# Graph attention on one core: the last chunk of 32 slots is prepared behind all adds of the chunk in front of it

## What is computed

```python
def _gat(x, src, dst, W, a_src, a_dst, b):
    n = x.shape[0]
    xw = (x @ W).reshape(n, H, FH)
    al_s = jnp.einsum('nhf,hf->nh', xw, a_src)
    al_d = jnp.einsum('nhf,hf->nh', xw, a_dst)
    e = jax.nn.leaky_relu(al_s[src] + al_d[dst], NEG_SLOPE)
    m = jax.ops.segment_max(e, dst, num_segments=n)
    ee = jnp.exp(e - m[dst])
    den = jax.ops.segment_sum(ee, dst, num_segments=n)
    alpha = ee / den[dst]
    out = jax.ops.segment_sum(alpha[:, :, None] * xw[src], dst, num_segments=n)
    return out.reshape(n, H * FH) + b
...
h = jax.nn.elu(_bn(_gat(x, src, dst, W1, a1_src, a1_dst, b1), g1, beta1))
h = jax.nn.elu(_bn(_gat(h, src, dst, W2, a2_src, a2_dst, b2), g2, beta2))
```

## Time and profile before

| what | value |
|---|---|
| median of 3 runs | 5546.97 us (5546.96 to 5551.64) |
| the profiled execution's own time | 5593.81 us |
| its span | 5592.0 us |
| first attention layer, first to last add | 2846.4 to 4111.4 us |
| second attention layer, first to last add | 4260.7 to 5523.4 us |

### The profile page before, as it was taken

One profiled execution on the slowest core, in us unless ns is written; L12 is line 12 of the kernel. 1 busy time (PEld: TensorE's weight loads), 2 busy tenths in 40 slices (PEclk: granted clock), 3 DMA queues, 4 the chain that ended last, 5 costly groups with the idle time before them and its releaser, 6 DMA issues.

```text
span 5592.0 us, 63654 instructions
## 1 busy us (share of the span) xinstructions
PE 3147.6 (56%) x12887; PEld 2272.1 (41%) x12887; DVE 2561.5 (46%) x9589; ACT 1064.3 (19%) x2505; POOL 3194.9 (57%) x3310
## 2 busy tenths in 40 slices
PE   7946666676734444444415555655651555555555
PEld 3434333343423333333314444444540444444444
DVE  6433333333333443444515555555571555555557
ACT  3301111121200000000102222222230222222223
POOL 0166666666266666666466666666526666666651
PEclk9957777777855555555555555555565555555556
DMA  6513333333322222222122222222102222222221
GB/s 238 228 44 111 124 121 118 118 119 123 115 71 53 55 54 54 55 54 56 35 48 45 45 45 45 45 45 45 39 26 49 46 44 45 45 45 45 45 43 47
DMA packets 168746, 395.78 MB, mean 71 GB/s; under 512 B 57590, under 2 KB 92468, under 8 KB 151092
## 3 DMA queue, kind: packets, MB, share of 16 engines
q0 software_dynamic: 103872, 215.70, 16.8%
q10 hardware_dynamic: 37968, 103.60, 4.8%
q1 hardware_dynamic: 26532, 72.39, 3.5%
HBM read 230.11 MB, written 161.35 MB: 70 GB/s over the span
## 4 chain that ended last, share of the span: by engine, by line
PE 34%; issue 22%; another core or an unknown queue 21%; DVE 13%; ACT 3%; POOL 2%; DVEq 2%; DMA 1%; SPq 1%; ACTq 0%; POOLq 0%
PE B L1770 9%; PE B L1650 8%; PE B L1550 6%; DVE AC L1033 3%; PE B L1612 3%; DVE AC L852 3%; PE B L1705 2%; PE B L1719 2%; ACT hold L1376 1%; POOL Gr L1889 1%; DVE Sr L937 1%; DVEq L308 1%; POOL Gr L1872 1%; DVE Sr L840 1%
## 5 line engine op out<-in xcount | busy, mean ns | idle before, releaser
L1889 POOL DMA_INDIRECT Gr<-Gtab,SRC x1664 | 1617.4, 972 | 1010.6 <-issue 471.4
L1872 POOL DMA_INDIRECT Gr<-Ttab,GID x1568 | 1501.8, 958 | 1045.6 <-issue 413.4
L1650 PE MATMUL B<-Gr,Sr 128*128 x3328 | 916.8, 402 | 723.7 <-issue 381.3
L1770 PE MATMUL B<-Gr,Sr 128*128 128x136 f32 x3328 | 1059.8, 462 | 402.2 <-DVE AC L1033 187.8
L1650 PEld LDWEIGHTS B<-Gr,Sr 128*128 128x128 f32 x3328 | 742.0, 279 | 1104.2 <-issue 1100.0
L1033 DVE TENSOR_TENSOR AC<-AC,B 128x136 f32 x1664 | 486.9, 293 | 1135.1 <-PE B L1770 470.8
L1770 PEld LDWEIGHTS B<-Gr,Sr 128*128 128x128 f32 x3328 | 786.4, 304 | 520.5 <-issue 243.6
L852 DVE TENSOR_TENSOR AC<-AC,B 128x128 f32 x1664 | 476.3, 286 | 937.8 <-remote 400.2
L1550 PE MATMUL B<-XW,hT 128*128 128x512 f32 x672 | 474.5, 798 | 90.3 <-ACT Sr L1202 32.9
L1705 PE MATMUL B<-identb,hold 128*128 128x128 bf16 x1664 | 251.9, 305 | 464.3 <-ACT hold L1376 259.5
L840 DVE TENSOR_SCALAR Sr<-iota,DL 128x128 f32<-128x128 f32 x1664 | 494.3, 299 | 15.8 <-issue 10.9
(11 more groups left out here) (275 smaller groups left out, 2358.2 us busy)
## 6 DMA issues: line engine op xcount, KB each, us to landing
Ttab<-Sr ACTq DMA_DIRECT2D x84, 1024.0 KB
Ttab<-Sr SPq DMA_DIRECT2D x51, 1024.0 KB
Gr<-Gtab,SRC POOLq DMA_INDIRECT x1664
Gr<-Ttab,GID POOLq DMA_INDIRECT x1568
Gtab<-Gr ACTq DMA_DIRECT2D x84, 66.0 KB
X1D<-Gr ACTq DMA_DIRECT2D x84, 64.0 KB
Gtab<-XW SPq DMA_DIRECT2D x7, 462.0 KB, 3.7
out<-Sr SPq DMA_DIRECT2D x12, 256.0 KB
```

The lines of the kernel that those rows point to most:

```text
L1650: e.matmul(B[banks[s % len(banks)]][:, 0:P], selr(s), Gr[:, bass.ds(o, P)], start=True, stop=True).then_inc(slot_mm, 1)
L1770: e.matmul(B[s % 3][:, 0:CW], sel(s), Gr[:, (s % GR) * CW:(s % GR + 1) * CW], start=True, stop=True).then_inc(gat_mm, 1)
L1872: e.indirect_dma_start(out=Gr[:, (sn + 1) % TG * P:((sn + 1) % TG + 1) * P], out_offset=None, in_=Tt[L][:, :], in_offset=bass.IndirectOffs ...
L1889: e.indirect_dma_start(out=Gr[:, (s % GR) * CW:(s % GR) * CW + 132], out_offset=None, in_=T2[L][0:NPAD][:, :], in_offset=bass.IndirectOffs ...
```

## The change

In chunk 24, the chunk in front of the last, VectorE and TensorE take no turn of `prep(25)` at the even steps from 14. What is left of it after the first twelve turns runs in `finish(gen)`, behind step 31. All other chunks are as they were, and ScalarE, GpSimd and SyncE have the same program.

```diff
@@ gat_vector @@
                 for i in range(CH):
                     s = c * CH + i
                     if c + 1 < NC and i % 8 == 4 and i < 24:
                         weigh(c, i // 8 + 1)
                     if s >= LAG:
                         add(s - LAG)
-                    if i < 12 or (i >= 14 and i % 2 == 0):
+                    if i < 12 or (i >= 14 and i % 2 == 0 and c + 2 < NC):
                         next(gen, None)
                 finish(gen)
                 if c + 1 < NC:
                     weigh(c + 1, 0)
```

## The result

The changed kernel takes 5559.35 us (median of 18 runs, 5551.64 to 5571.57), the kernel before 5547.72 (18 runs, 5543.56 to 5564.19). The ratio is 1.0017, with a 95% interval of 1.0010 to 1.0025, so the change costs about 9.4 us (5.5 to 13.9); the two medians are 11.6 us apart. The forecast was 5560.4.

The account below looks back on a forecast made before the run. After the last gather, VectorE's adds and chunk 25's weights were taken to set the layer's end; exposed chain 4.0 + 4.25 plus GpSimd's hold-up 5.2 gave 13.4 us, so 5546.97 became 5560.4 us, range 5552 to 5567.

Parts of the forecast that it names:

- Step 1: Chunk 24 on VectorE: 17 adds, a register load and a weighing take 10.27 us from slot 12's add to slot 29's.
- Step 2: Chunk 24 on TensorE: the chain's first transpose comes 10.5 us behind the add of slot 12.
- Step 3: Chain for chunk 25 with nothing between: 9.0 us, from 5.92 (chunk 0's rows), 3.04 (chunk 24's) and 0.04.
- the clock: TensorE's granted clock may be lower in chunk 25; costed at nothing, as adds keep their pace.
- Step 4: Weighing of piece 0 of chunk 25: 4.0 us later in the first layer, 4.25 in the second, together 8.2.
- Step 5: Start of chunk 25: GpSimd's multiplies hold up L1026 by 0.70 and L1028 by 1.9 us, 5.2 in all.
- Rival A: Start of chunk 25: chain exposed, but L1026 and L1028 not held up; +8.2 us, 5555.2 us, chance 0.36.
- Rival B: Bare chain in chunk 24 stalls as chunk 0's does, 4.4 and 3.8 us more; 5568.6 us, chance 0.17.
- Rival C: Kernel gets faster: the chain would have to take under 5 us or the 17 adds under 6; chance 0.03.

Follow-up runs that it names:

- q_before: The kernel before with 22 added idle-result reductions of 128x1024 on VectorE in each of chunks 0 to 23: 5651.21 us.
- p_before: The kernel before with 11 added idle-result reductions of 128x1024 on VectorE in each of chunks 0 to 23: 4658.97 us.
- b_again: The kernel before, without any edit, run again for its trace on another chip: 4653.93 us.
- e2_gps_late: The kernel before, but GpSimd's three multiplies of chunk 25 wait until VectorE has weighed piece 0: 4650.73 us, ratio 1.0009.
- q_after: The changed kernel with 22 added idle-result reductions of 128x1024 on VectorE in each of chunks 0 to 23: 5658.78 us.
- p_after: The changed kernel with 11 added idle-result reductions of 128x1024 on VectorE in each of chunks 0 to 23: 4657.81 us.
- a_again: The changed kernel, without any edit, run on the chip where the kernel before takes 4653.93 us: 4644.84 us, ratio 0.9981.
- e1_scale_psum: The changed kernel, but L1026 and L1028 of chunk 25 read their factor from PSUM: 4634.53 us against 4646.46 for the kernel before, ratio 0.9974.
- e5: The change made in all chunks, not in chunk 24 alone: 5883.71 us against 5546.12 for the kernel before, ratio 1.0617.

## Why the prediction came out as it did

| kernel | chip | W, first and second layer | S, first and second layer |
|---|---|---|---|
| before | A | 0.16, 0 | 21.58, 21.30 |
| q_before | A | 0.16, 0 | 21.27, 21.25 |
| p_before | C | 7.46, 4.36 | 28.83, 25.69 |
| b_again (before) | C | 10.21, 10.13 | 31.62, 31.19 |
| e2_gps_late (before, with the hold-up) | B | 9.91, 9.48 | 33.08, 32.63 |
| after | A | | 26.93, 27.16 |
| q_after | A | | 27.69, 28.31 |
| p_after | C | | 27.31, 27.16 |
| a_again (after) | C | | 27.45, 27.23 |
| e1_scale_psum | B | | 24.92, 24.64 |

(W is left out where the order is the changed one; it is 0.2 to 0.8 us there.) With the order before, S is 21.4 + W in each of the first eight cases, within 0.35 us, and 1.8 more in e2_gps_late, by the hold-up that its edit brings. With the changed order it is 26.9 to 27.7 on chips A and C, and 28.3 once; without the hold-up, in e1_scale_psum, it is 2.3 less. So the change costs 5.8 us a layer where the gathers are early and gains as soon as VectorE waits more than 5.8 us for them. This gives e1 its sign too: with W at 9.7 the order before has 31.1 on chip B, and 31.1 less 24.8 is 6.3 us a layer, 12.6 in all, for the 12 measured.

*Step 1, the adds:* forecast 10.27 from the add of slot 12 to that of slot 29; measured 10.25 in both layers.

*Step 2, the chain's start:* forecast 10.5; measured 10.43 in both.

*Step 3, the bare chain:* forecast 9.0, measured 8.45 and 8.65. The second half was right (L995 to the weighing 3.03 for 3.08). The first half was sized on chunk 0's rows, where the first transpose takes 0.47 and the half 5.92; here it takes 0.27 and the half 5.42 and 5.62. The difference is TensorE's granted clock. In chunk 0, after 30.12 us without work, it is 0.50 of full speed (1.2 GHz) at both pairs of transposes (L1726 and L1727, L1733 and L1734). Here the first pair follows the products without a gap and has 1.00 (2.4 GHz) in both layers; the second pair has 1.00 in the first layer and 0.50 in the second. The clock is the third number from the end of a row, here of chunk 0's first pair in the kernel before, then of the first layer's first pair and the second layer's second pair in the kernel after:

```profile
2817.90:2818.80 0.90, 0.69 (x2) 0.29 (x2) 0.00 (x0) 0.12 (x2) 0.60 (x2) 0.50 0.21 47
```

```profile
4058.70:4059.20 0.50, 0.47 (x4) 0.23 (x3) 0.50 (x2) 0.00 (x0) 0.00 (x0) 1.00 0.00 0
...
5472.30:5472.90 0.60, 0.58 (x2) 0.09 (x2) 0.00 (x0) 0.00 (x0) 0.00 (x0) 0.50 0.00 0
```

From L1726 to L948 it takes 0.82 and 0.83 us here and 1.12 in chunk 0; from L1733 to L963 0.70 in the first layer, and 0.91 in the second and in chunk 0. These two stretches are the whole difference of that half. The prediction costed the clock at nothing because adds don't depend on it; the chain does. Of the steps this is the term that was mis-sized, by 0.9 in the two layers.

*Step 4, the sum to the weighing:* forecast +4.0 and +4.25, measured +3.4 and +3.8.

*Step 5, the hold-up by GpSimd:* forecast 0.70 and 1.9 a layer, measured 0.61 for L1026 and 1.70 for L1028. Rival A, that small instructions slip through, is refuted by e1 and e2: the hold-up comes and goes with the place of the factor and with the time of the multiplies.

Altogether 13.4 was forecast, the trace has 11.8, and the ratio says 9.4, with 13.4 inside its interval. So the mechanism stood. That the time was only 1 us off is partly luck: the sum was 1.6 us above the trace's, the interval of the measured cost is 8.4 us wide, and the kernel before came out at 5547.72 and not at 5546.97. The prediction leaned to slower by over 0.2% (0.54 against 0.43 for within); the ratio says 0.17%, with 0.2% inside its interval, so 18 runs don't decide between the two.

*Rival B* did not occur in chunk 24: with the gathers over, the bare chain had no stall. In e5, where the bare chain stands beside running gathers, stalls did occur, and each chunk costs twice the chain.

*Rival C is where the prediction was blind.* It said that a gain would need the chain to be under 5 us or the adds under 6, and gave 0.03. That was right for the trace shown and wrong as a statement on the kernel. The sum that would have shown it was at hand. GpSimd issues a gather each 1.25 us (0.95 and 0.30 idle), 40 us a chunk, and chunk 24, with no gathers left, took VectorE 32.6 us (from the weighing of its piece 0 at 4058.47 to that of chunk 25 at 4091.03). So an unhindered core is paced by the gathers, and then the last gather lands after step 14. That is what chip C shows: its first 25 chunks take 41.1 us each in the first layer, and the first copy that needs a chunk's rows waits for the gathers in all 52 preparations (b_again):

```profile
ACT hold L1387 <- DMA Gr<-Gtab,SRC: 549.9, 52, 34.6
```

In the kernel before on chip A, the chunks take 49.9 us each, and that copy waits for a gather in chunk 0 of each layer alone:

```profile
ACT hold L1387 <- DMA Gr<-Gtab,SRC: 61.5, 2, 31.8
```

There the engines lost more than the difference of 7.4 us to waits that the trace puts down to nothing in the core, and the gathers had the lead. I read that lead as a property of the kernel.

## What to carry to other kernels

A step in an in-order queue that waits for a transfer holds up everything behind it, so its best place depends on whether the transfer has landed by then. Measure that wait in the trace: here moving the step back costs 5.8 us and saves the wait, and the wait is 0 on one chip and 10 us on another. Before a sum is trusted beyond one trace, compare the steady pace of the producer with that of the consumer (40 against 32.6 us a chunk): if the trace shows the slower one ahead, something outside the kernel is holding the other, and the sign may turn elsewhere. When work is moved so that it starts together with another engine's, look for instructions further down that now fall beside it; a small one with both inputs in SBUF, next to GpSimd's multiplies, cost 1.9 us instead of 0.16, and reading one input from PSUM removes that.

Of all versions the changed kernel with the factor in PSUM had the lowest ratio on the chips with late gathers (0.9974, against 0.9981 without it on the other such chip; the intervals overlap, and the two were not run on one chip). On chip A it was run only with padding, where it was slower than the order before; a version that is best on both kinds was not found.

## What was not expected

The same program takes 5548 us on one chip and 4650 on two others, 16% less. The chain that ended last has no share for outside waits on chip C:

```profile
PE 38%; DMA 15%; issue 14%; DVE 13%; POOL 12%; ACT 3%; DVEq 3%; SPq 1%; ACTq 0%; POOLq 0%
```

and 21% of them in the same kernel on chip A:

```profile
PE 34%; issue 22%; another core or an unknown queue 21%; DVE 13%; ACT 3%; POOL 2%; DVEq 2%; DMA 1%; SPq 1%; ACTq 0%; POOLq 0%
```

In its list of waits they are with several engines (us in total, times, longest):

```profile
ACT hold L1368 <- remote: 500.1, 69, 19.1
...
DVE AC L1033 <- remote: 456.7, 144, 24.8
...
DVE AC L852 <- remote: 400.2, 124, 12.2
```

The profile names no transfer, engine or queue of the core for them; what they are stays open. So it stays open too why VectorE is late on chip A: that its gathers are early follows from these waits, but no experiment took them away. Durations of single instructions are the same on all three chips (an add 0.30, a gather 0.95, a weighing 1.21).
